# Sandwich of attention and a mixture-of-experts layer: the last batch's gating, the experts' weight splits and the shared expert's down products reordered

## The chip, the cores and the metric

One Trainium2 chip, one core. The metric is the time of one execution on the device in microseconds, the median of several. All engines (TensorE or PE, VectorE or DVE, ScalarE or ACT, GpSimd or POOL, SyncE or SP) run instruction lists of their own, each in its order, and are tied by counting semaphores that the kernel writes by hand.

## The reference

What is computed, with x of 4 batches x 512 tokens x 256 features, all float32:

```python
x = x + layernorm(attention1(layernorm(x)))        # 16 heads of 16, causal
h = layernorm(x)                                   # "hidden_states" of the second layer
hid = h + attention2(rmsnorm(h, ln1_w))            # 16 heads of 128, causal
x2 = rmsnorm(hid, ln2_w)
logits = x2 @ gate_w.T                             # 16 experts
probs = softmax(logits)
top_w, top_i = top_k(probs, 4);  top_w /= sum(top_w)
g, u = x2 @ w1[e]                                  # per expert, 176 wide each
routed = sum_e wfull[t, e] * ((silu(g) * u) @ w2[e].T)
shared = (silu(x2 @ sg.T) * (x2 @ su.T)) @ sh_down_w.T   # shared expert, 352 wide
x = x + layernorm(hid + routed + shared)
```

The experts are evaluated only for the tokens that chose them.

## The kernel before

The work goes through five stages: first attention, second attention (64 steps of one head of one batch), the shared expert, the routed experts (79 tiles of 128 rows), and the last normalisation. The second attention's output is accumulated in `hs`. While it works on batch b, the kernel also does the gating of batch b-1 in fixed steps (the `POST_...` constants): the rms norm, the transposes of x2, the logits, the softmax, the ranks (each expert's probability is compared with every other's), the places in the sorted row table `xs_rows`, and the scattering of rows. For the last batch (B-1 = 3) there is no later attention, so its gating is woven into the shared expert.

The shared expert is a loop over `SHARED` = 12 steps s, that is 4 batches x `SHR` = 3 slices of 128, 128 and 96 hidden features. In a step

- TensorE computes the gate and the up product (`shared_up(s)`, 12 matmuls of 512 columns into bank s%2 and bank 2+s%2), and a down product (`shared_down`, 12 matmuls of 256 columns into banks 6 and 7). Products of float32 data are made of three, with each operand split in a high and a low part (`_hi`, `_lo`).
- ACT takes silu of the gate into `gated[s%2]` (L1004), DVE multiplies it with the up product (L1407), ACT rounds it to the high part `hh_hi` (L1008), and POOL (steps 1 to 5, `shared_lo`, L733) or DVE (steps 0 and 6 to 11, L1417) subtracts to get the low part `hh_lo`. The down product of a slice needs both parts. The silu of step s >= 2 waits until the down product of step s-2 is done (`f_dn` >= s-1), since it overwrites `gated[s%2]`.
- After three slices DVE adds the down products to `hs` (L1414), which first needs `f_dn`, and `r_row` (the rows of that batch copied out).

Into the same loop are laid: the splits of the experts' first weights w1 in four quarters (c, gu), each a `w1_half` on ACT (L996, 128 x 2816) and a `w1_rest` on DVE (L1398, 128 x 2816, reading the raw and the high part in SBUF); and the last batch's gating: `norm_half` on ACT (L917) and `norm_half2` on DVE (L1245) write the normalised rows into `mid`, TensorE transposes them (`turn_x2`, L1709), ACT and DVE make xT from them (`take_x2`, L922 and L1250), TensorE does `logits` (L1716), DVE `logits_less_max` (L1258 to L1261), ACT `exp_logits` (L926), DVE `probabilities`, `compare` and `count_ranks` (L1265 to L1288), TensorE `counts` (L1731), DVE `places`, `rows_and_weights` (L1294 to L1315) and `table` (L1322 to L1334), which TensorE transposes (L1894) and DVE stores as `tab` (L1441).

POOL's list is not touched by the change: `root_of_squares`, `shared_lo(1)` to `(5)`, and then `send_tile` for the last batch's four tiles (tiles 12 to 15). A `send_tile` waits for the indices (`r_idx`), the weights (`r_w`) and the row fill of its tile (`r_row`, `fill_row` on ACT, L935), does two small copies (L681, L682) and issues four indirect DMAs (L684) that scatter rows to `xs_rows`. `fill_row` of tile 14 overwrites the buffer of tile 12 and waits until its four DMAs have landed; tile 15 waits for 13's.

SP loads the second expert weights w2 in four parts (`load_w2`, which wait for `f_u`); then waits for `tab` and for all rows sent (`x_sent`), loads tiles 0 to 3, the last part of w2, and then tiles 4 to 78 in turn. An expert tile goes through `turn_tile`, `take_x`, `up`, silu, `turn_h` and `down`; TensorE's loop does `up(i)`, `down(i-2)`, `turn_h(i-1)`, `turn_tile(i+2)`. The first `up` also waits for all four `w1_rest`, and the first `take_x` on ACT for the last down product (`f_dn` >= 12).

The order of everything in the loop is written out by hand with tests on s.

Of the kernel before, what the change touches and what calls it, by code (L numbers as in the profile page):

```python
# [31 lines left out]
def sandwich_kernel(nc, x_d, qkv1_d, wo1_d, qkvo2_d, ln_w_d, gate_d, moe_d, stack_d, out_d):  # L32
    B, TB, D = x_d.shape
    C = D // P
# [6 lines left out]
    E = gate_d.shape[2]  # L41
# [8 lines left out]
    SHR = -(-SHI // P)  # L50
# [22 lines left out]
    with ctx:  # L73
# [6 lines left out]
        bank = [ctx.enter_context(nc.psum_tensor(f"bank{i}", [P, 512], F32)) for i in range(8)]  # L80
# [248 lines left out]
        POST_ROW, POST_SEND = (11, 12, 13, 14), (12, 13, 14, 15)  # L329
        SHARED = B * SHR  # L330
        LO_POOL = 6

        def sends(when, n):

# [2 lines left out]
        def shared_rows(r):  # L337
            return min(P, SHI - P * r)
# [138 lines left out]
        def _(pool):  # L477
# [258 lines left out]
            root_of_squares(B - 1)  # L736
            for s in range(1, LO_POOL):
                shared_lo(s)
# [12 lines left out]
        def _(act):  # L751
# [168 lines left out]
            def take_x2(b, c, bank_):  # L920
                act.wait_ge(r_tp2, b * C + c + 1)
                act.activation(xT[:, b, HI, c, :], bank_[:, :], ACT.Copy, scale=ln_w[:, 1, c:c + 1]).then_inc(r_hi, 1)  # L922

            def exp_logits(b):
                act.wait_ge(r_sub, b + 1)
                act.activation(pr[:, :, :], lg[:, :, :], ACT.Exp).then_inc(r_exp, 1)  # L926

            def fill_row(b, j):

                t = TPB * b + j  # L930
                if t == 0:
                    act.wait_ge(d_const, 1)
                if t >= 2:
                    act.wait_ge(x_sent[t % 2], 16 * TOPK * (t // 2))
                act.activation(xrow[:, t % 2, :, 0:D], hs[:, t, :].unsqueeze(1).to_broadcast([P, TOPK, D]), ACT.Copy,  # L935
                               scale=midst[:, RR, j:j + 1]).then_inc(r_row, 1)
# [56 lines left out]
            def w1_half(c, gu):  # L993

                act.wait_ge(w_in[c], 16 * len(list(routed_pieces(gu, c))) * 2)
                act.activation(w1[HI][c][:, gu, :], w1_raw[c][:, gu, :], ACT.Copy, scale=ln_w[:, 1, c:c + 1])\  # L996
                   .then_inc(w_hi, 1)

            for s in range(SHARED):
                rows = shared_rows(s % SHR)  # L1000
                act.wait_ge(f_g, s + 1)
                if s >= 2:
                    act.wait_ge(f_dn, s - 1)
                act.activation(gated[0:rows, s % 2, :], bank[s % 2][0:rows, :], ACT.Silu).then_inc(f_silu, 1)  # L1004
                if s == 3:
                    exp_logits(B - 1)
                act.wait_ge(f_h, s + 1)
                act.activation(hh_hi[0:rows, s % 2, :], gated[0:rows, s % 2, :], ACT.Copy).then_inc(f_hh, 1)  # L1008
                if s == 0:
                    w1_half(0, 0)  # L1010
                    norm_half(B - 1)
                if s == 1:
                    for c in range(C):
                        take_x2(B - 1, c, bank[4 + c])
                    w1_half(0, 1)
                if s in (6, 7):
                    w1_half(1, s - 6)
                if s in (5, 6, 7, 8):
                    fill_row(B - 1, s - 5)

            def take_x(i):
                act.wait_ge(e_t, i + 1)
# [30 lines left out]
        def _(dve):  # L1053
# [202 lines left out]
            def logits_less_max(b, bank_):  # L1256
                dve.wait_ge(r_lg, b + 1)
                link(dve.tensor_reduce(lg[:, :, :], bank_[:, 0:2 * TPB * E].rearrange("p (t a e) -> p t e a", t=TPB, a=2),  # L1258
                                       AX.X, ALU.add))
                link(dve.tensor_reduce(col[:, :], lg[:, :, :], AX.X, ALU.max))  # L1260
                dve.tensor_tensor(lg[:, :, :], lg[:, :, :], wide(col[:, :]), ALU.subtract).then_inc(r_sub, 1)  # L1261

            def probabilities(b):
                dve.wait_ge(r_exp, b + 1)
                link(dve.tensor_reduce(col[:, :], pr[:, :, :], AX.X, ALU.add))  # L1265
                link(dve.reciprocal(col[:, :], col[:, :]))
                link(dve.tensor_tensor(pr[:, :, :], pr[:, :, :], wide(col[:, :]), ALU.mult))

            def compare(experts):

                above = []
                for e in experts:
                    own = pr[:, :, e:e + 1]
                    if e:
                        above.append(dve.tensor_tensor(rk[:, :, e, 0:e], pr[:, :, 0:e],
                                                       own.to_broadcast([P, TPB, e]), ALU.is_ge))
                    above.append(dve.tensor_tensor(rk[:, :, e, e:E], pr[:, :, e:E],
                                                   own.to_broadcast([P, TPB, E - e]), ALU.is_gt))
                link(*above)
# [116 lines left out]
            def w1_rest(c, gu):  # L1396
                dve.wait_ge(w_hi, 2 * c + gu + 1)
                dve.scalar_tensor_tensor(w1[LO][c][:, gu, :], w1_raw[c][:, gu, :], ln_w[:, 1, c:c + 1], f32(w1[HI][c][:, gu, :]),  # L1398
                                         ALU.mult, ALU.subtract).then_inc(w_lo, 1)

            for s in range(SHARED + 1):
                if s < SHARED:
                    rows = shared_rows(s % SHR)
                    dve.wait_ge(f_silu, s + 1)
                    dve.wait_ge(f_u, s + 1)
                    half = gated[0:rows, s % 2, :]
                    dve.tensor_tensor(half, half, bank[2 + s % 2][0:rows, :], ALU.mult).then_inc(f_h, 1)  # L1407
                if s and s % SHR == 0:
                    b = s // SHR - 1
                    dve.wait_ge(f_dn, s)  # L1410
                    dve.wait_ge(r_row, TPB * (b + 1))
                    for i in range(2):
                        two = hs[:, TPB * b + 2 * i:TPB * b + 2 * i + 2, :].rearrange("p j d -> p (j d)")
                        dve.tensor_tensor(two, two, bank[6 + i][:, :], ALU.add).then_inc(f_acc, 1)  # L1414
                if s == 0 or LO_POOL <= s < SHARED:
                    dve.wait_ge(f_hh, s + 1)
                    dve.tensor_tensor(hh_lo[0:rows, s % 2, :], gated[0:rows, s % 2, :], f32(hh_hi[0:rows, s % 2, :]),  # L1417
                                      ALU.subtract).then_inc(f_lod, 1)
                if s == 0:
                    norm_half2(B - 1)  # L1420
                if s == 1:
                    for c in range(C):
                        take_x2(B - 1, c, bank[4 + c])
                    w1_rest(0, 0)
                if s == 2:
                    logits_less_max(B - 1, bank[4])
                    w1_rest(0, 1)
                if s == 3:
                    probabilities(B - 1)
                    compare(range(0, 6))  # L1430
                if s == 4:
                    compare(range(6, E))
                    count_ranks(B - 1)
                if s == 5:
                    places(B - 1, bank[5])
                    rows_and_weights(B - 1)
                if s == 6:
                    table()
                if s == 7:
                    dve.wait_ge(r_tabT, 1)  # L1440
                    dve.tensor_copy(tab[0:1, :], bank[4][0:1, 0:2 * P]).then_inc(r_tabi, 1)  # L1441
                if s >= SHARED - 2 and s < SHARED:
                    w1_rest(1, s - SHARED + 2)

            def take_x(i):
                dve.wait_ge(e_xh, i + 1)
# [49 lines left out]
        def _(pe):  # L1496
# [375 lines left out]
                ins.then_inc(f_dn, 1)  # L1872

            pe.wait_ge(s_ok, SHR)
            for s in range(SHARED + 1):
                if s == SHR * (B - 1):
                    pe.wait_ge(r_lo, C * B)
                if s < SHARED:
                    shared_up(s)
                if s:  # L1880
                    shared_down(s - 1)
                if s == 1:
                    pe.wait_ge(b_acc, C * N2)
                    for c in range(C):
                        turn_x2(B - 1, c, bank[4 + c])
                if s == 2:
                    logits(B - 1, bank[4])
                if s == 5:
                    pe.wait_ge(r_lo, C * B)
                    counts(B - 1, bank[5])  # L1890
                if s == 7:
                    pe.wait_ge(r_tab, 1)
                    for i in range(2):
                        ins = pe.transpose(bank[4][0:1, P * i:P * (i + 1)], tabc[:, i:i + 1], ident[:, :])  # L1894
                    ins.then_inc(r_tabT, 1)
# [131 lines left out]
```

## Time and profile before

| | us |
|---|---|
| median of 3 runs | 1220.91 |
| lowest, highest | 1219.78, 1225.69 |
| the profiled execution's own time | 1221.95 |
| its span, first to last instruction | 1220.2 |

| engine | busy us | share of the span | instructions |
|---|---|---|---|
| TensorE matmuls | 1160.6 | 95% | 7868 |
| DVE | 846.3 | 69% | 2663 |
| ACT | 799.6 | 66% | 2069 |
| POOL | 580.7 | 48% | 844 |

Times of the profile are microseconds from the first instruction. A row of a timeline gives the start, the duration, the engine, the line of the kernel and the operation, then output <- input tiles, and in brackets how long the engine had been idle and what ended that. A line L1500 is that of a helper that issues nearly all matmuls. The shared expert runs from 923.6 us to about 991 us, the expert tiles follow. Durations of instructions that follow each other at once overlap by up to 0.1 us.

### The profile page before, as it was taken

The page shows a single profiled execution, that of the slowest core. Times are in us where ns is not written, and L with a number is a line of the kernel's source. Part 1 is how long each engine was busy: PE and PEld are TensorE (multiplying, and loading weights), DVE is VectorE, ACT ScalarE, POOL GpSimd, SP SyncE. Part 2 cuts the span into 40 slices and gives each one's busy share as a digit, 9 for nine tenths or more (in the row PEclk, how much of TensorE's full clock was granted, in tenths as well). Part 3 has the DMA queues.
Part 4 walks back from the last instruction along what each step waited for, and adds up shares of the span by engine and source line. Part 5 has one row for each costly group of instructions (what it writes and reads, how often), then busy time and mean ns, then how long its engine had stood idle before and what let it go on. Part 6 is the DMA issues. An engine that isn't in the chain of part 4 may idle for free.

```text
span 1220.2 us, 25017 instructions
## 1 busy us (share of the span) xinstructions
PE 1160.6 (95%) x7868; PEld 988.4 (81%) x7868; DVE 846.3 (69%) x2663; ACT 799.6 (66%) x2069; POOL 580.7 (48%) x844
## 2 busy tenths in 40 slices
PE   6999999899999999999999999999998879999986
PEld 5766566689999989999989999889986769999962
DVE  5778888576677667876677876668865755555535
ACT  3587888677778776778776787777786524444422
POOL 4063655454334444457343466334453446666650
PEclk9999999999999999999999999999999989999998
DMA  8965555256631211213121131211114237777766
GB/s 271 284 190 168 173 175 170 89 176 191 189 114 57 91 51 57 81 53 123 35 69 37 35 109 67 69 36 54 64 54 132 78 112 116 118 119 118 119 110 223
DMA packets 111779, 139.58 MB, mean 114 GB/s; under 512 B 11364, under 2 KB 94820, under 8 KB 111524
## 3 DMA queue, kind: packets, MB, share of 16 engines
q1 hardware_dynamic: 97204, 119.10, 32.2%
q0 software_dynamic: 14448, 18.88, 9.5%
q8 instruction: 68, 1.11, 0.4%
q14 instruction: 59, 0.48, 0.1%
HBM read 63.36 MB, written 61.87 MB: 103 GB/s over the span
## 4 chain that ended last, share of the span: by engine, by line
PE 76%; DVE 8%; ACT 6%; issue 4%; POOL 3%; DMA 2%; SPq 1%; POOLq 0%; ACTq 0%; DVEq 0%
PE bank L1500 56%; PE bank L1742 5%; PE bank L1926 5%; PE bank L1561 2%; DVE bank L1127 2%; PE bank L1597 2%; PE bank L1614 2%; POOL xs_rows L684 1%; PE bank L1604 1%; PE bank L1905 1%; PE bank L1936 1%; ACT pT L842 1%; POOL sum_rows L746 1%; ACT p L966 1%; DVE hs L1358 1%
## 5 line engine op out<-in xcount | busy, mean ns | idle before, releaser
L1127 DVE CUSTOM_DVE_ANT_0 bank<-bank,mask 128x512 f32<-128x512 f32 (+3 forms) x512 | 235.1, 522 | 42.3 <-PE bank L1500 21.6
L957 ACT ACTIVATE p<-bank,stat 128x512 f32<-128x512 f32 (+3 forms) x256 | 131.6, 527 | 127.0 <-DVE stat L1127 127.0
L537 POOL CAST w_hl<-raw_qkv 128x512 fp32r<-128x512 f32 x96 | 58.8, 613 | 301.9 <-DMA raw_qkv<-in_qkvo 154.2
L1500 PE MATMUL bank<-xT,w_hl 128*128 128x512 f32 x768 | 190.3, 396 | 0.0
L1500 PEld LDWEIGHTS bank<-xT,w_hl 128*128 128x128 f32 x768 | 142.2, 188 | 37.1 <-issue 2.0
L746 POOL DMA_INDIRECT sum_rows<-mid,goal x79 | 122.9, 1555 | 70.7 <-DVE mid L1464 68.1
L966 ACT ACTIVATE p<-p,stat 128x512 f32<-128x512 f32 (+3 forms) x256 | 123.1, 553 | 14.7 <-DVE stat L1361 14.7
L538 POOL TENSOR_TENSOR w_hl<-raw_qkv,w_hl 128x512 fp32r<-128x512 f32 x96 | 124.2, 1294 | 7.8
L1383 DVE TENSOR_TENSOR o<-bank,o 128x512 fp32r<-128x512 f32 x64 | 44.2, 690 | 109.4 <-ACT o L973 109.4
L1500 PE MATMUL bank<-pT,v 128*128 128x256 f32 (+2 forms) x576 | 117.1, 348 | 0.0
L1500 PE MATMUL bank<-k,q 128*128 128x512 f32 (+2 forms) x576 | 111.5, 337 | 2.5 <-ACT pT L950 1.7
L1500 PE MATMUL bank<-wo_hl,o 128*128 128x256 f32 x768 | 107.6, 289 | 3.6 <-DVE o L1383 1.4
L1500 PEld LDWEIGHTS bank<-w_hl,xT 128*128 128x128 f32 x768 | 98.7, 188 | 10.7 <-issue 5.5
L1500 PEld LDWEIGHTS bank<-k,q 128*128 128x128 f32 x576 | 96.9, 189 | 11.7 <-DVE k L1231 1.9
L1500 PE MATMUL bank<-w_hl,xT 128*128 128x256 f32 x768 | 101.4, 280 | 3.1 <-DVE xT L1250 3.1
L1500 PEld LDWEIGHTS bank<-wo_hl,o 128*128 128x128 f32 x768 | 95.9, 190 | 5.5 <-issue 3.2
L842 ACT ACTIVATE pT<-bank 128x512 f32<-128x512 f32 x160 | 85.3, 603 | 19.0 <-PE bank L1604 17.4
L1500 PE MATMUL bank<-w_hi,sh_hi 128*128 x316 | 96.9, 348 | 0.5 <-issue 0.4
L1345 DVE TENSOR_TENSOR pT<-bank,pT 128x256 fp32r<-128x256 f32 (+2 forms) x192 | 96.1, 550 | 0.4
L1500 PEld LDWEIGHTS bank<-pT,v 128*128 128x128 f32 x576 | 87.9, 189 | 3.2
L524 POOL TENSOR_SCALAR_AFFINE_SELECT pT<-pT 128x256 f32<-128x256 f32 x128 | 51.5, 407 | 70.2 <-ACT pT L842 65.7
L1358 DVE TENSOR_TENSOR hs<-hs,bank 128x512 f32<-128x512 f32 x128 | 81.9, 679 | 1.1 <-PE bank L1500 1.1
(248 smaller groups left out, 2561.3 us busy)
## 6 DMA issues: line engine op xcount, KB each, us to landing
raw_qkv<-in_qkvo SPq DMA_DIRECT2D x32, 768.0 KB, 5.3
xs_rows<-blank SPq DMA_DIRECT2D x32, 520.0 KB, 3.3
xs_rows<-blank SPq DMA_DIRECT2D x5, 2730.0 KB, 14.6
xrow<-xs_rows SPq DMA_DIRECT2D x79, 130.0 KB, 2.5
raw_o<-in_qkvo SPq DMA_DIRECT2D x32, 256.0 KB, 3.6
sum_rows<-blank SPq DMA_DIRECT2D x3, 2176.0 KB, 8.5
stk<-xT SPq DMA_DIRECT2D x96, 64.0 KB
stk<-k_hl SPq DMA_DIRECT2D x96, 64.0 KB
```

The source lines that it names most:

```text
L537: link(pool.tensor_copy(hi, raw))
L538: pool.tensor_tensor(lo, raw, f32(hi), ALU.subtract).then_inc(done, 1)
L746: pool.indirect_dma_start(sum_d[i % NSUM], bass.IndirectOffsetOnAxis(goal[:, i % NY:i % NY + 1], 0), yt[:, i % NY, :], None, compute_op=AL ...
L842: act.activation(pT1[:, s % 2, i, :], st1(s, i)[:, :], ACT.Exp).then_inc(a1_exp, 1)
L957: act.activation(p2[:, n % 2, POFF[qi]:POFF[qi + 1]], s2(t), ACT.Exp, scale=-1.0, bias=stat2[:, 0, n % 2, t:t + 1], accum_out=stat2[:, 1, ...
L966: act.activation(pt, pt, ACT.Copy, scale=stat2[:, 2, n % 2, t:t + 1]).then_inc(b_norm, 1)
L1127: return dve.tensor_tensor_reduce(scores, scores, mask[:, TB - scores.shape[1]:], scale=-1.0, scalar=-2.0 * MASKED, op0=ALU.add, op1=ALU.m ...
L1345: dve.tensor_tensor(pT2[:, LO, QOFF[kj]:QOFF[kj + 1]], bank[t][:, 0:TB - P * kj], f32(pT2[:, HI, QOFF[kj]:QOFF[kj + 1]]), ALU.subtract).th ...
L1358: dve.tensor_tensor(two, two, bank[4 + c][:, :], ALU.add).then_inc(b_acc, 1)
L1500: ins = pe.matmul(out, a, b, start=start and i == 0, stop=stop and i == len(pairs) - 1, **kw)
L1742: ins = pe.transpose(bank[t][:, P * (qi - kj):P * (qi - kj + 1)], p2[:, (n - 1) % 2, POFF[qi] + P * kj:POFF[qi] + P * (kj + 1)], ident[:, :])
L1926: ins = pe.matmul(bank[6 + i % 2][:, 0:D], ht[:, i % 2, P * h:P * (h + 1)], w2r[:, ds(expert[i], 1), h, :].rearrange("p a n -> p (a n)"), ...
```

## The change

It reorders the lists of TensorE, ACT and DVE in the shared expert's loop; no instruction is added or taken away.

- TensorE: the down product of a slice is issued two steps after its up product instead of one (the loop has a step more); the last batch's transposes move from step 1 to step 2, behind `shared_down(0)`; its logits move from step 2 to step 3, and stand ahead of `shared_down(1)`.
- ACT: `norm_half` from step 0 to step 1; `take_x2` from step 1 to step 2, now between silu and the rounding; `exp_logits` stays in step 3 but goes ahead of that step's silu; the four `w1_half` go from steps 0, 1, 6, 7 to steps 2, 4, 7, 8; the row fills from steps 5, 6, 7, 8 to 5, 6, 8, 9.
- DVE: `take_x2` from step 1 to step 2; `logits_less_max`, `probabilities` and the first compares stand at the head of step 3, the other compares and the count at the head of step 4, ahead of the products; the additions to `hs` move a step later; the four `w1_rest` go from steps 1, 2, 10, 11 to steps 7, 8, 9, 10.

```diff
+        SPLIT_W1, REST_W1, FILL_LAST = (2, 4, 7, 8), (7, 8, 9, 10), (5, 6, 8, 9)
...
             for s in range(SHARED):                                   # ACT
                 rows = shared_rows(s % SHR)
+                if s == 3:
+                    exp_logits(B - 1)
                 act.wait_ge(f_g, s + 1)
                 if s >= 2:
                     act.wait_ge(f_dn, s - 1)
                 act.activation(gated[...], bank[s % 2][...], ACT.Silu).then_inc(f_silu, 1)
-                if s == 3:
-                    exp_logits(B - 1)
+                if s == 2:
+                    for c in range(C):
+                        take_x2(B - 1, c, bank[4 + c])
                 act.wait_ge(f_h, s + 1)
                 act.activation(hh_hi[...], gated[...], ACT.Copy).then_inc(f_hh, 1)
-                if s == 0:
-                    w1_half(0, 0)
+                if s == 1:
                     norm_half(B - 1)
-                if s == 1:
-                    for c in range(C):
-                        take_x2(B - 1, c, bank[4 + c])
-                    w1_half(0, 1)
-                if s in (6, 7):
-                    w1_half(1, s - 6)
-                if s in (5, 6, 7, 8):
-                    fill_row(B - 1, s - 5)
+                if s in SPLIT_W1:
+                    w1_half(*divmod(SPLIT_W1.index(s), 2))
+                if s in FILL_LAST:
+                    fill_row(B - 1, FILL_LAST.index(s))
...
-            for s in range(SHARED + 1):                               # DVE
+            for s in range(SHARED + 2):
+                if s == 3:
+                    logits_less_max(B - 1, bank[4])
+                    probabilities(B - 1)
+                    compare(range(0, 6))
+                if s == 4:
+                    compare(range(6, E))
+                    count_ranks(B - 1)
                 if s < SHARED:
                     ...
-                if s and s % SHR == 0:
+                if s > SHR and s % SHR == 1:
                     b = s // SHR - 1
-                    dve.wait_ge(f_dn, s)
+                    dve.wait_ge(f_dn, s - 1)
...
-                if s == 1:
+                if s == 2:
                     for c in range(C):
                         take_x2(B - 1, c, bank[4 + c])
-                    w1_rest(0, 0)
-                if s == 2:
-                    logits_less_max(B - 1, bank[4])
-                    w1_rest(0, 1)
-                if s == 3:
-                    probabilities(B - 1)
-                    compare(range(0, 6))
-                if s == 4:
-                    compare(range(6, E))
-                    count_ranks(B - 1)
...
-                if s >= SHARED - 2 and s < SHARED:
-                    w1_rest(1, s - SHARED + 2)
+                if s in REST_W1:
+                    w1_rest(*divmod(REST_W1.index(s), 2))
...
-            for s in range(SHARED + 1):                               # TensorE
+            for s in range(SHARED + 2):
                 if s == SHR * (B - 1):
                     pe.wait_ge(r_lo, C * B)
                 if s < SHARED:
                     shared_up(s)
-                if s:
-                    shared_down(s - 1)
-                if s == 1:
+                if s == 3:
+                    logits(B - 1, bank[4])
+                if s >= 2:
+                    shared_down(s - 2)
+                if s == 2:
                     pe.wait_ge(b_acc, C * N2)
                     for c in range(C):
                         turn_x2(B - 1, c, bank[4 + c])
-                if s == 2:
-                    logits(B - 1, bank[4])
```

## Rows read from the trace of the kernel before

**Rows 1.** the chain of waits from 955 to 1003 us: start us, us, what

```profile
961.88 0.20 POOL xrow L681
...
985.89 2.44 DMA xs_rows<-xrow,idx
...
998.96 2.07 DMA xrow<-xs_rows
```

**Rows 2.** one line of the kernel, the sends: duration ns min/median/max

```profile
L684 POOL DMA_INDIRECT xs_rows<-xrow,idx x64: 956/964/3827, 538.5 to 985.9; - x64
```

**Rows 3.** POOL timeline, 920 to 1006: start, us, engine line op, tiles, [idle before]

```profile
939.80 4.16 POOL L733 TENSOR_TENSOR hh_lo<-gated,hh_hi 96x512 fp32r<-96x512 f32 x1 [5.04 <-ACT hh_hi L1008]
...
972.97 0.20 POOL L681 COPY xrow<-dst 128x4 int32<-128x4 int32 x1
...
979.01 1.17 POOL L684 DMA_INDIRECT xs_rows<-xrow,idx  x1 [0.28 <-POOL xrow L682]
...
981.76 3.83 POOL L684 DMA_INDIRECT xs_rows<-xrow,idx  x1 [0.30 <-issue]
```

**Rows 4.** DVE timeline, 920 to 1006

```profile
930.61 0.61 DVE L1245 TENSOR_SCALAR mid<-hs,midst 128x256 f32<-128x256 f32 x2 [1.78 <-POOL midst L673]
...
938.98 0.28 DVE L1258 TENSOR_REDUCE lg<-bank 128x64 f32<-128x128 f32 x1
...
946.94 0.21 DVE L1265 TENSOR_REDUCE col<-pr 128x4 f32<-128x64 f32 x1
...
950.79 0.18 DVE L1275 TENSOR_TENSOR ranks<-pr 128x24 bf16<-128x24 f32 x1
...
951.72 1.31 DVE L1277 TENSOR_TENSOR ranks<-pr 128x24 bf16<-128x24 f32 x1
...
955.54 0.19 DVE L1288 TENSOR_SCALAR msk<-lg 128x64 bf16<-128x64 f32 x1
...
961.58 0.17 DVE L1315 TENSOR_TENSOR wk<-posf,col 128x16 f32<-128x16 f32 x1
...
964.07 0.41 DVE L1322 TENSOR_TENSOR ranks<-run,thr 128x256 f32<-128x256 f32 x1
...
967.50 0.69 DVE L1407 TENSOR_TENSOR gated<-gated,bank 128x512 f32<-128x512 f32 x1
...
978.64 0.68 DVE L1417 TENSOR_TENSOR hh_lo<-gated,hh_hi 128x512 fp32r<-128x512 f32 x1
...
981.60 3.15 DVE L1398 SCALAR_TENSOR_TENSOR w_lo<-w_raw,ln_w,w_hi 128x2816 fp32r<-128x2816 f32 x1
...
989.71 1.27 DVE L1414 TENSOR_TENSOR hs<-hs,bank 128x512 f32<-128x512 f32 x2
```

**Rows 5.** ACT timeline, 920 to 1006

```profile
930.61 0.91 ACT L917 ACTIVATE mid<-hs,midst 128x256 f32<-128x256 f32 x2
...
962.39 0.63 ACT L1008 ACTIVATE hh_hi<-gated 128x512 fp32r<-128x512 f32 x1 [3.87 <-DVE gated L1407]
962.93 2.63 ACT L996 ACTIVATE w_hi<-w_raw,ln_w 128x2816 fp32r<-128x2816 f32 x1
...
971.29 1.13 ACT L935 ACTIVATE xrow<-hs,midst 128x1024 f32<-128x1024 f32 x1
```

**Rows 6.** ACT timeline, 1160 to 1221

```profile
1176.81 1.28 ACT L757 ACT_TABLE_LOAD   x1
```

**Rows 7.** TensorE timeline, 920 to 1006

```profile
944.01 0.38 PE L1500 MATMUL bank<-sh_hi,hh_hi 96*128 96x256 f32 x1 [2.56 <-POOL hh_lo L733]
...
967.76 0.48 PE L1500 MATMUL bank<-xT,sh_hi 128*96 128x512 f32 x1
...
970.61 0.28 PE L1500 MATMUL bank<-sh_hi,hh_hi 128*128 128x256 f32 x1
...
972.04 0.40 PE L1500 MATMUL bank<-xT,sh_hi 128*128 128x512 f32 x1
```

**Rows 8.** windows: stretch, busy us (count) of each engine, granted TensorE clock, DMA

```profile
945.50:949.00 3.50, 3.50 (x11) 2.73 (x10) 3.06 (x16) 1.88 (x2) 0.00 (x0) 0.51 0.00 0
```

## The prediction

> **What bounds the kernel now.** I read four views, in this order. First the page: TensorE is busy 95% of the span and leads the chain that ended last, but that is an average, and the change lies between the end of the second attention (922 us) and the first expert tiles. Second, the chain of waits of that stretch. From 961.88 to 985.89 us it is not TensorE but POOL, which issues the 16 scattering DMAs of the last batch (`send_tile`); the last one lands at 985.89 + 2.44 = 988.33, then SP issues four tile loads, the last weight loads and the load of tile 4, which lands at 998.96 + 2.07 = 1001.03, and from there TensorE runs tile after tile [rows 1]. So 12.7 us after the last send lands the steady expert loop begins, and the end of the sends sets the end of the kernel. Third, the timelines of POOL, DVE and ACT, for what releases the first send (`wk` on DVE, 961.58 [rows 4]) and what stretches the sends. Fourth, the windows, for TensorE's clock.
>
> What stretches a send: 64 of them take 0.964 us in the median and 3.83 at most [rows 2]. The long one starts at 981.76, 0.16 us after a `w1_rest` on DVE (981.60, 3.15 us, both tensor inputs in SBUF), and ends at 985.59, 0.84 us after that ends [rows 3, 4]. The same sum fits a small case: `hh_lo` on DVE ends at 979.32, the send that starts at 979.01 ends at 980.18, 0.86 us later. A POOL subtraction issued while `w1_rest(0,1)` runs (939.80) takes 4.16 us. I take the rule: a send that starts inside such a DVE operation ends 0.85 us after it, so each `w1_rest` among the sends costs 1.75 to 3.0 us (its 3.15 less up to 1.27, the spacing of sends, less 0.12), 2.4 on the average.
>
> The Trainium skill ("SBUF — State Buffer", section "SBUF: two separate sides") says that the port pair shared by DVE and GpSimd is an exclusive lock, taken by a DVE operation with two SBUF inputs against a GpSimd one that reads SBUF, and held for the whole instruction by whichever starts first. The stretched sends agree. By the same rule a `w1_rest` that meets a running send would wait up to one send (0.96) itself, which would add up to 1 us to the sum; this trace shows no such wait, so the sum leaves it out.
>
> **The change part by part.** Times below are those of the profiled execution. An `up` of TensorE takes 2.74 to 2.85 us, a `down` 1.43 [rows 7]; silu 0.58, the product on DVE 0.69, `hh_hi` 0.63, `w1_half` 2.63, a row fill 1.13, each 0.05 to 0.09 shorter where the next follows at once [rows 4, 5].
>
> *Up to the logits (even).* The first w1 half leaves ACT (it held norm_half until 930.61), but norm_half now stands behind `hh_hi` of step 1, which needs the product of step 1, and that is queued on DVE behind norm_half2 (930.61 + 0.61). So product 931.1 to 931.8, `hh_hi` to 932.5, norm_half to 933.3 instead of 931.5: 1.8 us later [rows 4, 5]. TensorE spends this time on up 2 and down 0 (to 933.4), then the transposes, then up 3 (to 937.05). ACT and DVE take x2 by 936.15 (before 935.4), the logits follow up 3 at once, and less-max starts at 938.94 against 938.98 [rows 4]. Cost nothing; up 3 is the cover, and without it the step would be 0.8 late.
>
> *From logits to ranks (gain 7.9).* Now the exponential comes before silu 3 and the probabilities before product 3. With the table loaded while ACT waits (at the end of the kernel the load stands at 1176.81, long before its instruction's data [rows 6]) (1.28 us) it ends at 940.0, 0.3 behind less-max, and DVE goes on at once. Before, product 3, the slow POOL subtraction (939.80 + 4.16, since `w1_rest` ran beside it), a TensorE stall and the addition to hs stood between, until 946.94 [rows 3 to 5]. After: probabilities and the first compares 940.04 to 941.9, product 3 when silu 3 is through its own table load (942.3 to 942.9), the other compares and the count 4.9 (950.79 to 955.73, in it 1.1 that one compare waits for POOL, 1.31 long among others of 0.18 [rows 4]): ranks at 947.8, before 955.73. The moved downs cost nothing here: TensorE runs gapless from 934 to 957, and the slow stretch at 945.5 (granted clock 0.51, the 1.2 GHz level, after the stall [rows 7, 8]) goes.
>
> *From ranks to the first send (4.5 given back).* Counts can start at 948.6, but DVE's product 4 and addition end at 949.6 and product 5 needs silu 5, and that is behind `w1_half(0,1)`, which step 4 now holds (949.0 to 951.6). A product, the places, rows and weights take 6.0 us (955.73 to 961.58 + 0.17 [rows 4]), so from silu 5's end at 952.2 they end at 958.3. The first send moves from 961.88 to 958.4: **3.4 us earlier**.
>
> *The sends (8.0 lost).* Before: 24.97 us, of it one lock of 2.86, so 22.1 free. All four `w1_rest` now stand at steps 7 to 10, all inside the sends; two were at 935 and 939, one after the sends. The table (964.07 to 967.50, 3.4 us [rows 4]) now ends at 963.7. TensorE has nothing to do between down 5 (957.2) and the transposes of the table at 963.8, 6.6 us; after the stall of 2.56 us that ended at 944.01 [rows 7] it ran 3.5 us at half clock, so up 8 will run slow, 2.85 + 0.9 to 2.4. Then down 6 ends near 970.2, and silu 8 now waits for it. Product 8 ends at 971.5, `hh_hi` at 972.1, `w1_half(1,1)` 974.7, fill 2 at 975.8. POOL: tile 12's sends 958.4 to 964.0, tile 13's 964.0 to 971.6 (one lock, `w1_rest(0,0)` at 966.4), then it waits for fill 2 until 975.9 (before, fill 2 ended at 971.29 + 1.13, just in time for tile 14's copies at 972.97 [rows 3, 5]). Two tiles free are 10.8 us (972.97 to 986.85 less 2.86 and 0.2), and `w1_rest(1,0)` near 978.3 and `w1_rest(1,1)` near 983.7 fall into them, 2.4 each: the last send ends at 975.9 + 10.8 + 4.8 = 991.5 instead of 986.85.
>
> **Sum: +4.6 us**: the chain behind the sends (SP's loads, 12.7 us) moves as it is. TensorE's own last `down` ends near 990 and DVE's last addition near 991.5 (before 989.71 + 1.27), both hidden behind the tile loads, which would arrive at 996. By bounds: with the full clock at up 8, fill 2 ends at 974.4 and the sends at 990.1 (+3.3); with half clock throughout up 8 and locks as long as the measured 2.86, +6.2. The profiled execution took 1221.95 against a median of 1220.91; I add to the median: **1225.5 us**.
>
> **The rivals.** *Locks absent (not slower).* If the 3.83 send had another cause (it is one case), only the wait for fill 2 is left: 974.4 to 975.9 plus 10.8 gives 985.2 to 986.7, -1.6 to -0.2: about 1220. For it: the long send is one case, and the median of 64 shows none. Against: the end 0.85 after DVE's fits twice. It decides from where the two locks behind fill 2 cost under 0.2 to 1.7 us together (986.85 less 10.8 less 975.9 or 974.4).
>
> *Everything late (slower by over 0.5%).* The exponential's table load does not run ahead (+1.3 at the ranks, +0.9 at fill 2), up 8 wholly at half clock (+1) and locks of 2.86 (+0.9): +7.5, 1228.4. For it: [rows 6] is another load, at another place. Against: like it, the exponential has a single wait.
>
> *Sends no longer the bound (faster).* If fill 2 came in time and DVE's `w1_rest` mostly missed the sends (starts of sends just ahead of them), POOL would end at 958.4 + 22.1 = 980.5, and the first expert tile would be held by DVE's last addition, 991.5, instead of the load at 991.5, then three tiles of 2.27 without waits: `up` 3 at about 998.7 instead of 1001.9, -3.2, 1217.7. It needs silu 8 not to wait for down 6, against the order.
>
> *The change does nothing there* is excluded: order alone moves 3.4 us at the first send.
>
> **How the numbers follow.** Forecast (+3.3 to +6.2) 0.57; locks absent 0.14; all late 0.18; sends not the bound 0.07; something I don't see that makes it faster by more 0.04. Half a per cent is 6.1 us, about what a measurement can tell from no change. All late is slower; the forecast, locks absent and sends not the bound lie within. So faster 0.04, same 0.78, slower 0.18. The range leaves out the far ends of both sides, 1218.5 to 1228.5 (half of sends not the bound, the unseen, and the upper part of all late, together under 2 in 10); the forecast's own is 1224.2 to 1227.1.
>
> **What would show it.** Right: less-max at about 938.9; ranks near 947.8; first send near 958.4; a TensorE gap of 6 us ahead of the table's transposes and a granted clock near 0.5 in the 3 to 5 us behind them; three or four sends over 2.5 us, each ending 0.85 after a `w1_rest`; POOL idle on `xrow` of fill 2; last send near 991.5. Wrong: sends of 0.96 beside `w1_rest`, fill 2 before 972, or a first expert `up` that waits for DVE instead of a load.

## The result and the profile after

Six runs of the changed kernel took 1229.97 us in the median (1228.83 to 1231.23), six of the kernel before 1220.78. The ratio is 1.0068, with 95% interval 1.0050 to 1.0087: slower by 0.68%, or 8 to 9 us, against a forecast of 4.6. The time lies 1.5 us above the range's upper end. The direction and most of the mechanism were right, the size was not.

The profiled execution of after took 1228.98 us (span 1227.2, mean granted clock 0.984, against 0.990 before), 7.0 us more in the span. The first product of the shared expert starts at 926.19 us (before 926.75), and times after it are compared from that product. In the 13 profiles of this document it starts between 925.80 and 928.47, though nothing ahead of it was edited; this scatter stands in the medians and not in times from the product. The first view is the chain that ended last (start us, us, what):

```profile
973.54 2.16 ACT w_hi L997
...
975.99 1.15 ACT xrow L936
977.28 0.19 POOL xrow L682
...
980.86 2.76 POOL xs_rows L685
...
985.22 3.07 POOL xrow L683
...
992.64 2.44 DMA xs_rows<-xrow,idx
...
1005.83 2.16 DMA xrow<-xs_rows
```

As in [rows 1], it goes through POOL's sends, SP's loads and the load of tile 4. The new piece is ahead of them: POOL now stands behind ACT's `w1_half(1,1)` (L997) and fill 2, the row fill of tile 14 (L936). POOL's timeline (start, us, engine line op, tiles, idle before):

```profile
968.04 3.04 POOL L685 DMA_INDIRECT xs_rows<-xrow,idx  x1 [0.30 <-issue]
...
977.28 0.19 POOL L682 COPY xrow<-dst 128x4 int32<-128x4 int32 x1 [4.92 <-ACT xrow L936]
...
979.30 1.26 POOL L685 DMA_INDIRECT xs_rows<-xrow,idx  x1 [0.30 <-issue]
980.86 2.76 POOL L685 DMA_INDIRECT xs_rows<-xrow,idx  x1 [0.30 <-issue]
...
985.17 3.11 POOL L683 COPY xrow<-wk 128x4 f32<-128x4 f32 x1
...
989.85 1.21 POOL L685 DMA_INDIRECT xs_rows<-xrow,idx  x1 [0.30 <-issue]
```

Three long spans answer to the one of [rows 3], and one of them is a copy of 4 elements a partition, which takes 0.19 elsewhere. DVE's timeline shows what each meets; `w1_rest(0,1)`, at 974.18 and not among these rows, falls into POOL's wait and holds nothing:

```profile
938.42 0.29 DVE L1257 TENSOR_REDUCE lg<-bank 128x64 f32<-128x128 f32 x1 [2.76 <-PE bank L1496]
...
947.30 0.19 DVE L1287 TENSOR_SCALAR msk<-lg 128x64 bf16<-128x64 f32 x1
...
948.00 1.27 DVE L1420 TENSOR_TENSOR hs<-hs,bank 128x512 f32<-128x512 f32 x2
953.04 0.68 DVE L1413 TENSOR_TENSOR gated<-gated,bank 96x512 f32<-96x512 f32 x1 [3.77 <-ACT gated L1007]
...
967.11 3.13 DVE L1397 SCALAR_TENSOR_TENSOR w_lo<-w_raw,ln_w,w_hi 128x2816 fp32r<-128x2816 f32 x1
...
979.63 3.15 DVE L1397 SCALAR_TENSOR_TENSOR w_lo<-w_raw,ln_w,w_hi 128x2816 fp32r<-128x2816 f32 x1
...
985.09 3.14 DVE L1397 SCALAR_TENSOR_TENSOR w_lo<-w_raw,ln_w,w_hi 128x2816 fp32r<-128x2816 f32 x1
```

The send at 968.04 ends at 971.08, 0.84 after the `w1_rest` that ends at 970.24; the one at 980.86 ends at 983.62, 0.84 after 982.78. The copy at 985.17 ends at 988.28, 0.05 after 988.23: a held copy needs no 0.85. TensorE's timeline has two stalls, and the windows (stretch; busy us of PE, PEld, DVE, ACT, POOL; granted clock; DMA share, GB/s) show the 1.2 GHz level behind both:

```profile
949.42 0.55 PE L1496 MATMUL bank<-sh_hi,hh_hi 128*128 128x256 f32 x1 [2.55 <-DVE hs L1420]
...
964.50 0.58 PE L1890 MATMUL bank<-ident,tabc 128*1 128x128 f32 x2 [3.42 <-DVE tabc L1333]
```

```profile
949.40:952.30 2.90, 2.88 (x15) 2.81 (x15) 0.00 (x0) 1.88 (x1) 0.71 (x1) 0.50 0.50 145
964.50:969.90 5.40, 5.40 (x15) 3.62 (x16) 5.40 (x6) 3.16 (x2) 4.51 (x6) 0.52 0.21 75
```

Added up from the first product on, the last send ends at +67.41 (before +60.10). The 7.31 are 2.04 gained at the first send's copies, 4.92 of waiting for fill 2, 4.27 more of held instructions, that is what sends and copies took beyond their usual 0.97 and 0.19 (7.57 in all, before 3.30) and 0.16 of small gaps. Tile 4's transposes come at +81.85 (before +74.33, so +7.52), and from there to the end both take the same: 219.16 and 219.12.

### The profile page after: what moved, and what is told of

The parts are those of the page before. It is cut to its first block, busy times and chain, and to the rows that moved or that the text cites. A ratio compares the mean times of both kernels' runs of the same rounds, so it can differ in the third digit from the quotient of the medians.

```text
span 1227.2 us, 25017 instructions
## 1 busy us (share of the span) xinstructions
PE 1163.8 (95%) x7868; PEld 991.6 (81%) x7868; DVE 846.5 (69%) x2663; ACT 799.6 (65%) x2069; POOL 581.7 (47%) x844
## 4 chain that ended last, share of the span: by engine, by line
PE 79%; DVE 9%; ACT 6%; issue 3%; DMA 2%; POOL 2%; SPq 1%; POOLq 0%; ACTq 0%; DVEq 0%
PE bank L1496 57%; PE bank L1738 5%; PE bank L1922 5%; PE bank L1557 2%; DVE bank L1126 2%; PE bank L1610 2%; PE bank L1593 2%; PE bank L1901 1%; PE bank L1600 1%; PE bank L1932 1%; ACT pT L843 1%; ACT p L967 1%; ACT stk L848 1%; DVE hs L1357 1%; POOL xs_rows L685 1%
```

## The experiments

Theories on record before the runs: the sends bound the kernel and are lengthened by the wait for fill 2 and by `w1_rest` (theory S); against it, the moved down products cost the time (T), or the slower clock alone. A lock is a `w1_rest` that holds up POOL. The table holds one profiled execution each, us from the first product; "held" is the excess of sends and of copies, "add" the end of the last addition to `hs`, "tile 4" its transposes. From there to the end it took 216.9 to 219.4 us, in e2_fill2_at7 221.0, so differences of tile 4 under 2 us need the medians. Most of that scatter is not in the tiles: from tile 4's transposes to the last `turn_h` it took 174.2 to 174.9 us in eleven of the profiles and 176.5 in e2_fill2_at7 and e3_table_at8, while the last stage behind it took 42.1 to 44.5.

| kernel | 1st copies | wait, fill 2 | held | sends end | add | tile 4 | ratio to before, 95% |
|---|---|---|---|---|---|---|---|
| before | 35.13 | 0 | 3.25+0.05 | 60.10 | 64.23 | 74.33 | |
| after | 33.09 | 4.92 | 4.50+3.07 | 67.41 | 68.33 | 81.85 | 1.0068, 1.0050 to 1.0087 |
| e1_rest_out | 33.85 | 6.19 | 3.55+2.88 | 68.30 | 66.10 | 82.77 | 1.0079, 1.0048 to 1.0110 |
| e2_fill2_at7 | 33.09 | 0 | 10.21+0.03 | 65.03 | 67.68 | 79.39 | 1.0067, 1.0043 to 1.0091 |
| e3_table_at8 | 33.03 | 2.88 | 4.07+3.31 | 64.98 | 64.65 | 79.31 | 1.0053, 1.0034 to 1.0072 |
| e4_rest_pieces | 31.89 | 4.85 | 4.47+0.35 | 63.20 | 68.23 | 77.52 | 1.0036, 1.0023 to 1.0048 |
| e5_add_early | 30.55 | 4.52 | 4.46+3.08 | 64.46 | 65.39 | 78.78 | 1.0041, 1.0023 to 1.0058 |
| e6_down_only | 36.32 | 0 | 0.18+0.07 | 58.24 | 68.55 | 75.50 | 0.9997, 0.9983 to 1.0011 |
| e7_splits_only | 31.09 | 0 | 5.31+5.65 | 63.75 | 64.43 | 78.35 | 1.0022, 1.0008 to 1.0037 |
| e8_no_locks | 31.92 | 1.81 (fill 3) | 0.38+0.02 | 55.94 | 67.27 | 78.55 | 1.0039, 1.0022 to 1.0057 |
| h1_best | 30.59 | 0 | 1.84+0.04 | 54.18 | 64.10 | 71.77 | 0.9968, 0.9954 to 0.9982 |
| h2_rest_at8 | 30.59 | 0 | 4.67+3.50 | 60.47 | 60.82 | 74.79 | 1.0010, 0.9995 to 1.0024 |
| h3_rest_back | 30.54 | 0 | 4.09+6.15 | 62.48 | 63.03 | 76.87 | 1.0042, 1.0027 to 1.0058 |

The intervals of e1_rest_out, e2_fill2_at7 and e3_table_at8 overlap widely with that of after, and that of e5_add_early at its end: what these edits did is read from the traces, and the medians alone do not show a gain.

**Four edits of after, one suspected cost each.** The first takes two `w1_rest` out of the sends' time:

```diff
-        SPLIT_W1, REST_W1, FILL_LAST = (2, 4, 7, 8), (7, 8, 9, 10), (5, 6, 8, 9)
+        SPLIT_W1, REST_W1, FILL_LAST = (0, 2, 7, 8), (2, 4, 10, 11), (5, 6, 8, 9)
```

> The changed kernel with SPLIT_W1 = (0, 2, 7, 8) and REST_W1 = (2, 4, 10, 11): two of the four w1_rest leave the sends, one comes late in them. Theory S (the end of the 16 sends on POOL sets the time; w1_rest locks POOL; POOL waits for fill 2): fill 2 stays at about 977, but behind it there is one lock instead of two to four, so the last send ends near 990.5 instead of 993.6, about 1227 us against 1230. Rival T (the cost is TensorE's: its stalls and the half-clock stretches of the down products a step later): those stay, so 1230.

It missed: 1230.02 us. Both late `w1_rest` met POOL all the same, because POOL still waited for fill 2 (6.19 us) and sent later. POOL's timeline, then DVE's:

```profile
937.09 1.30 POOL L734 TENSOR_TENSOR hh_lo<-gated,hh_hi 96x512 fp32r<-96x512 f32 x1 [2.10 <-ACT hh_hi L1012]
...
984.71 3.05 POOL L682 COPY xrow<-dst 128x4 int32<-128x4 int32 x1
...
989.46 4.15 POOL L685 DMA_INDIRECT xs_rows<-xrow,idx  x1 [0.30 <-issue]
```

```profile
937.28 4.06 DVE L1397 SCALAR_TENSOR_TENSOR w_lo<-w_raw,ln_w,w_hi 128x2816 fp32r<-128x2816 f32 x1
...
989.62 3.14 DVE L1397 SCALAR_TENSOR_TENSOR w_lo<-w_raw,ln_w,w_hi 128x2816 fp32r<-128x2816 f32 x1
```

The early `w1_rest` shows the other direction: POOL's subtraction had begun 0.19 before it, kept its 1.30, and DVE took 4.06, 0.92 more than 3.14. At 989.46 a send had begun 0.16 before DVE, and it is the send that was held, 4.15. "SBUF — State Buffer" of the Trainium skill (section "SBUF: two separate sides") says that whichever of the two starts first keeps the ports shared by DVE and GpSimd for its whole instruction. The subtraction agrees with that, the send does not.

```diff
-        SPLIT_W1, REST_W1, FILL_LAST = (2, 4, 7, 8), (7, 8, 9, 10), (5, 6, 8, 9)
+        SPLIT_W1, REST_W1, FILL_LAST = (2, 4, 7, 8), (7, 8, 9, 10), (5, 6, 7, 9)
```

> The changed kernel with the fill of tile 14 at step 7 instead of 8, all else equal. Theory S: POOL's wait of 4.9 us for fill 2 goes, a w1_rest now meets the sends of tile 14 (2.4 us back): about -2.5, 1227.5 us. Rival T: no change on TensorE, 1230.

The wait of 4.92 went, but now all four `w1_rest` met a send (10.21 us), so only 2.4 came back at the end of the sends: a wait and the locks are not two separate costs. The median (1230.46) shows no gain at all. The profile shows one reason: the tail from tile 4 took 221.03 instead of 219.16, and the clock fell once more in the expert tiles (window of this kernel, then the same stretch of after), where 1.6 of the difference lies:

```profile
1010.00:1015.00 5.00, 5.00 (x24) 4.29 (x24) 2.11 (x7) 1.63 (x5) 1.59 (x1) 0.72 0.53 114
```

```profile
1010.00:1015.00 5.00, 5.00 (x32) 4.59 (x31) 2.64 (x8) 2.25 (x7) 2.47 (x2) 1.00 0.72 139
```

The next kernel has such a fall too: a granted clock of 0.81 in the same window and 1.6 us more in the tiles. Its total from tile 4 does not show it (218.88), because its last stage took 42.3 us instead of 44.3.

```diff
-                if s == 7:            # transposes of the table, and its copy (two places)
+                if s == 8:
```

> The changed kernel with the table's transposes and its copy at step 8 instead of 7, so that TensorE does up 8 and down 6 while DVE makes the table. The 5 us stall of TensorE at 959.5 and the half clock behind it should go, silu 8 come 3.3 us earlier, fill 2 about 2 us earlier. Theory S: the sends follow fill 2, -2 us, about 1228. Rival T: all of the 5 us that up 8 and the stall cost comes back, 1225.

Moving the transposes behind up 8 took 2.04 of the wait and 2.5 at tile 4; 1228.37 us. TensorE's wait for the table did cost time at tile 4; that it costs time in the median is not shown.

```diff
-                dve.scalar_tensor_tensor(w1[LO][c][:, gu, :], ...).then_inc(w_lo, 1)
+                n = E * EI // 4
+                for i in range(4):
+                    some = slice(n * i, n * (i + 1))
+                    ins = dve.scalar_tensor_tensor(w1[LO][c][:, gu, some], ...)
+                ins.then_inc(w_lo, 1)
```

> The changed kernel with every w1_rest cut in four pieces of 704 columns (0.8 us each, some 0.3 us more in all). If POOL gets the port between two pieces, a send is held by at most one piece: theory S gives locks of under 0.9 instead of 1.8 to 3.1, about -3 us, 1227. If POOL doesn't get in between pieces, 1230, which would tell that the lock isn't given up between DVE instructions. Rival T: 1230 to 1231.

With 704 columns in place of 2816 the held copies went, 1225.83 us. The first held send did not get shorter: POOL's timeline, then DVE's, where the four pieces stand as one line:

```profile
966.46 3.43 POOL L685 DMA_INDIRECT xs_rows<-xrow,idx  x1 [0.30 <-issue]
...
979.60 1.42 POOL L685 DMA_INDIRECT xs_rows<-xrow,idx  x1 [0.31 <-issue]
```

```profile
965.51 3.52 DVE L1400 SCALAR_TENSOR_TENSOR w_lo<-w_raw,ln_w,w_hi 128x704 fp32r<-128x704 f32 x4
```

It stood through the rest of all four and ended 0.86 after them, while the later ones got through in 1.42. Of the 4.3 us gained at tile 4, 1.2 is not the edit's, as TensorE's timeline and window show:

```profile
949.06 0.36 PE L1500 MATMUL bank<-sh_hi,hh_hi 128*128 128x256 f32 x1 [2.57 <-DVE hs L1424]
949.25 0.28 PE L1500 MATMUL bank<-sh_hi,hh_lo 128*128 128x256 f32 x1
```

```profile
949.20:950.40 1.20, 1.20 (x11) 1.20 (x12) 0.00 (x0) 1.20 (x1) 0.55 (x1) 1.00 0.59 177
```

Down 3, the down product of step 3, starts behind the same stall as in after (2.57 us) and runs at full clock.

**The stall that the prediction missed.** The addition of batch 0 (`add_down`, the same two instructions) goes ahead of the rank count, and `w1_half(0,1)` into ACT's idle time before `hh_hi` of step 4:

```diff
                     compare(range(6, E))
+                    add_down(s)
                     count_ranks(B - 1)
...
-                if s > SHR and s % SHR == 1:
+                if s > SHR + 1 and s % SHR == 1:
```

> The changed kernel with the addition of batch 0's down products to hs ahead of the rank count (it stood behind it, and down 3 waits for it through f_acc: TensorE stood 2.55 us at 949.4 and ran at half clock behind it), and with w1_half(0,1) in ACT's gap before hh_hi of step 4. Theory S with the wait that I had missed: down 3 no longer waits, silu 5 comes 3 us earlier, the first send 2.4 us earlier (30.7 behind the first product instead of 33.1), and so do table and fill 2: about -2.5 us against the changed kernel, ratio to before about 1.0045. If the wait on the addition costs nothing, first send at 33.1 and 1.0068.

It hit: 1226.98 us, first send at +30.55 against 30.7. DVE's timeline:

```profile
946.98 1.28 DVE L1408 TENSOR_TENSOR hs<-hs,bank 128x512 f32<-128x512 f32 x2
...
951.58 0.68 DVE L1424 TENSOR_TENSOR gated<-gated,bank 96x512 f32<-96x512 f32 x1 [1.18 <-ACT gated L1007]
```

The mask of the ranks starts 1.2 later (+22.32 against +21.11 in after, the addition's 1.28), TensorE's wait ahead of down 3 shrinks from 2.55 to 0.46, and the first send comes 2.5 earlier, tile 4 by 3.1. The two edits were not run apart. The wait for fill 2 and the locks stay as in after.

**Single parts on the kernel before.** The downs and additions alone, and the splits alone:

```diff
-                if s and s % SHR == 0:
+                if s > SHR and s % SHR == 1:
-                    dve.wait_ge(f_dn, s)
+                    dve.wait_ge(f_dn, s - 1)
...
-                if s:
-                    shared_down(s - 1)
+                if s >= 2:
+                    shared_down(s - 2)
```

> The kernel before with only the down products (and the additions behind them) a step later. Rival T (the downs a step later cost TensorE stalls and half clock): slower by 3 us or more, ratio 1.003 or more. Theory S: the first send 1 to 2 us earlier, since the stall on hh_lo at 941 and the addition ahead of the probabilities go, one lock among the sends as before: ratio 0.999, between 0.998 and 1.001.

1221.55 us, no change, so T falls as the account of the whole. The stall is there in small: down 3 waits 1.32 us for the moved addition. That the ratio came out as expected is luck, since both steps behind it failed: the first send came 1.2 later and not 1 to 2 earlier, and the last two `w1_rest` came behind the sends, so nothing was held. The last send started at 983.80; DVE's timeline:

```profile
985.71 3.15 DVE L1398 SCALAR_TENSOR_TENSOR w_lo<-w_raw,ln_w,w_hi 128x2816 fp32r<-128x2816 f32 x1
...
993.81 1.27 DVE L1414 TENSOR_TENSOR hs<-hs,bank 128x512 f32<-128x512 f32 x2
```

The sends end 1.9 earlier than before and the time is the same: the addition, 4.3 later, has taken over, since DVE's first `take_x`, which TensorE's first `up` of the expert tiles needs, stands behind it, and tile 4 comes 1.2 later.

```diff
-                    w1_rest(0, 0)
...
-                    w1_rest(0, 1)
...
-                if s >= SHARED - 2 and s < SHARED:
-                    w1_rest(1, s - SHARED + 2)
+                if s in (7, 8, 9, 10):
+                    w1_rest(*divmod((7, 8, 9, 10).index(s), 2))
```

(and `w1_half` at steps 2, 4, 7 and 8)

> The kernel before with only the eight w1 splits moved to the changed kernel's steps (w1_half 2, 4, 7, 8; w1_rest 7, 8, 9, 10). Theory S: gating about 3 us earlier (DVE and POOL are free of w1_rest there), but four locks among the sends instead of one, some 6.5 us: +3 to +4 us, ratio 1.003, sends' locks 8 to 10 us in sum. Rival T: faster than before or even, as TensorE's order is the old one.

1224.87 us. The first send comes 4.0 earlier and the last ends 3.65 later, with no wait for fill 2. Each of the four meets POOL:

```profile
966.17 3.09 POOL L684 DMA_INDIRECT xs_rows<-xrow,idx  x1 [0.30 <-issue]
...
970.52 3.06 POOL L681 COPY xrow<-dst 128x4 int32<-128x4 int32 x1
...
976.55 3.85 POOL L684 DMA_INDIRECT xs_rows<-xrow,idx  x1 [0.30 <-issue]
...
981.68 2.97 POOL L681 COPY xrow<-dst 128x4 int32<-128x4 int32 x1
```

**Locks away, and the other bound.** After, with `SPLIT_W1, REST_W1, FILL_LAST = (0, 4, 7, 8), (1, 11, 12, 13), (5, 6, 7, 8)`:

> The changed kernel with no w1_rest among the sends (steps 1, 11, 12, 13; w1_half 0, 4, 7, 8) and the fills at 5 to 8. Times from the first product of the shared expert. Theory S: first send at about 33.1 as in the changed kernel, the 16 sends take 22.1 to 22.6 without a long one, last send end at 55 to 56 instead of 67.4; the kernel is then bound by DVE's three late w1_rest (about 9 us behind its last product), near the time before. If sends are stretched by something else than w1_rest (the rival that locks are absent), they take 25 us or more.

The sends ended at +55.94, where 55 to 56 was expected, 11.5 earlier than in after. Tile 4 came only 3.3 earlier and the kernel took 1226.48 us, not near the time before as expected, since DVE now has three `w1_rest` behind its products:

```profile
988.34 6.20 DVE L1397 SCALAR_TENSOR_TENSOR w_lo<-w_raw,ln_w,w_hi 128x2816 fp32r<-128x2816 f32 x2
994.47 1.27 DVE L1420 TENSOR_TENSOR hs<-hs,bank 128x512 f32<-128x512 f32 x2
995.66 3.14 DVE L1397 SCALAR_TENSOR_TENSOR w_lo<-w_raw,ln_w,w_hi 128x2816 fp32r<-128x2816 f32 x1
```

**A version that beats both.** e5_add_early, the table at step 8 as in e3_table_at8, and `(0, 4, 7, 8), (1, 7, 11, 12), (5, 6, 7, 8)`:

> The changed kernel with the addition and w1_half(0,1) as in e5, the table's transposes at step 8, the fills at 5 to 8, w1_half at 0, 4, 7, 8 and w1_rest at 1, 7, 11, 12: one w1_rest among the sends, one in a gap of DVE, two behind them. Theory S: first send 30.7 behind the first product, sends 22.1 free and one or two locks, last send end at 55 to 58 instead of 60.1 (before) and 67.4 (changed): faster than before by 2 to 5 us, ratio 0.996 to 0.998. The end of DVE's two last w1_rest and addition, at 62 to 64, may take over as the bound (it was 64.2 before); then -2. Rival T: the downs a step later keep it at or above 1.000.

1218.03 us, ratio to before 0.9968 (0.9954 to 0.9982). Eleven of its twelve executions took 1217.21 to 1220.34 us and one 1880.36, which no trace explains. One send is held and fill 2 is in time; DVE's two last `w1_rest` and the addition behind them are the bound, as the sends' end (+54.18) no longer is. POOL, then DVE, then the chain that ended last, which goes from DVE's additions over its first `take_x` (L1449) to the first `up` of the expert tiles:

```profile
965.99 2.69 POOL L685 DMA_INDIRECT xs_rows<-xrow,idx  x1 [0.30 <-issue]
...
979.82 0.97 POOL L685 DMA_INDIRECT xs_rows<-xrow,idx  x1 [0.31 <-issue]
```

```profile
964.69 3.15 DVE L1399 SCALAR_TENSOR_TENSOR w_lo<-w_raw,ln_w,w_hi 128x2816 fp32r<-128x2816 f32 x1
...
983.31 6.20 DVE L1399 SCALAR_TENSOR_TENSOR w_lo<-w_raw,ln_w,w_hi 128x2816 fp32r<-128x2816 f32 x2
```

```profile
983.31 6.20 DVE w_lo L1399 x2
989.51 1.20 DVE hs L1408 x2
990.71 0.35 DVE sh_hi L1449
...
991.19 2.12 PE bank L1502 x6
```

The same with `REST_W1` = (1, 7, 8, 12), to relieve DVE's end:

> As h1_best with the third w1_rest at step 8 (1, 7, 8, 12), where DVE stood idle for 3.15 us. One lock more among the sends (end 54.2 + 2.4 = 56.6), but DVE's tail 3 us shorter (add at 61 instead of 64.1). The sends are the bound again: tile 4 at about 70.8 instead of 71.8 or, by where full overlap starts, up to 2 us earlier than h1_best: ratio to before 0.995 to 0.997.

It missed, 1222.85 us: the `w1_rest` at step 8 held a copy (3.52), which moved the sends back until the last one met the `w1_rest` of step 12 (3.62). And with `REST_W1` = (7, 8, 9, 10) as in the changed kernel:

> As h1_best, but with the four w1_rest back at the changed kernel's steps 7, 8, 9, 10. It doubles the suspected cost alone in a kernel whose gating and fills are good: four locks, 7 to 10 us in sum, last send end at about 61 to 63 instead of 54.2, ratio to before near 1.000 to 1.002 (+4 us against h1_best). If the locks don't matter (rival T), the ratio stays at 0.997.

1225.23 us. Against h1_best only the places of the `w1_rest` differ, and the ratio to before goes from 0.9968 to 1.0042: 0.74% by them alone, with 8.4 us more of held instructions and no wait for fill 2 in either. In the profiles tile 4 comes 5.1 us later by it; the first product, ahead of all edits, came 1.8 later too, so a part of the 0.74% may be scatter.

## Why the prediction was wrong in size

**Up to the ranks: right.** From the first product on, less-max was forecast at 12.2 and came at 12.23. The exponential's table load did run ahead of its data, as ACT's timeline shows, and the mask of the ranks ended at 947.49, or +21.3, against +21.05.

```profile
937.86 1.28 ACT L927 ACT_TABLE_LOAD   x1
939.26 0.26 ACT L927 ACTIVATE pr<-lg 128x64 f32<-128x64 f32 x1
```

**Ranks to the first send: the step that failed.** The forecast said "The moved downs cost nothing here: TensorE runs gapless from 934 to 957". It followed the additions as work of DVE, but not as something TensorE waits for: down 3, the first of batch 1, needs banks 6 and 7 free (`f_acc`), and the addition that frees them now stands a step later, behind the rank count (948.00 to 949.27). TensorE idled 2.55 us and ran down 3 in 2.7 instead of 1.43. Silu 5 waits for down 3, as it overwrites that slice's `gated`, and stood 1.14 us beyond the end of `w1_half(0,1)`, which the forecast had taken as its only wait. ACT's timeline:

```profile
952.42 0.59 ACT L1007 ACTIVATE gated<-bank 96x512 f32<-96x512 f32 x1 [1.14 <-PE bank L1496]
```

Silu 5 ended at 953.01, product 5 began at 953.04, or +26.85 (forecast +25.5), and the send's copies at +33.09 (forecast +31.65): 1.4 late. e5_add_early, which takes away most of this wait and also `w1_half(0,1)` from ahead of silu 5, gave 2.5 us there; by the row above, at most some 1.1 of it is the addition's (an estimate).

**The wait for fill 2: right in kind, 1.9 late.** The transposes of the table came 1.25 late, as the first send did. Up 8 ran wholly at half clock, 5.14 us where the sum had taken 4.5: 0.64. Fill 2 ended at +50.94 against +49.05. POOL waited 4.92, forecast 4.3. TensorE's gap ahead of the transposes was 3.42 us and not 6.6, as TensorE came late out of the stall; the granted clock fell to 0.52 all the same.

**The locks: right, 0.8 too small.** Behind fill 2 they and the small gaps cost 5.6 instead of 4.8; the prediction priced sends alone, and a held copy loses 2.9 of the 3.1. The rule that a send ends 0.85 behind DVE's operation held in after four times, two of them beside short subtractions (971.08, 980.56, 983.62 and 991.06).

1.25, 0.64 and 0.77 are the 2.66 by which the last send missed its forecast of +64.75. That makes +7.3 in place of +4.6 at the sends. The forecast's upper bound of +6.2 had room for the slower up 8 and the longer locks; it had none for the 1.25, the stall that it had put at nothing. "Locks absent" is refuted by h3_rest_back, "sends no longer the bound" did not occur in after, but it is what e6_down_only, e8_no_locks and h1_best became. "Everything late" (+7.5) came nearest in size, in part by luck: two of its three terms were real (up 8 wholly at half clock, longer locks); the third, a late table load, was not, and the stall ahead of down 3 stood in its place.

**Open:** the medians differ by 9 us and the ratio by 8.3, the profile by 7.0; the 2.66 account for the profile alone. Three of the six runs of after lie at 1228.8 to 1229.4 (clock 0.983 and 0.984) and three at 1230.5 to 1231.2 (0.982 and 0.983). Three things that vary between single profiles are large enough for this: where the first product starts (by 2.7 us), the last stage (42.1 to 44.5 us), and the clock that falls again in the tiles (1.6 us, in e2_fill2_at7 and e3_table_at8). Which of them made the three slower runs no profile shows.

## What to carry to other kernels

When an addition out of an accumulator bank is moved, ask first who refills the bank: it is a wait of TensorE, and a stall can cost twice, by its length and by the clock behind it. Long DVE operations that read two SBUF tensors belong where POOL has nothing to send, and moving them moves the sends too, so check the new meetings and not the old ones. A stage with three limits (sends, a fill, the last addition) gives little for relieving one: e8_no_locks brought the sends forward by 11.5 us and tile 4 by 3.3.

## What the runs showed of the hardware that was not expected

- POOL's small copies are held like sends: 0.19 became 3.11 beside a `w1_rest` of 3.14.
- A send that began 0.16 before a `w1_rest` was held for 4.15, and DVE's operation kept its 3.14; POOL's subtraction that began 0.19 before kept its 1.30, and DVE took 4.06.
- Four shorter operations back to back need not let a send in: it was held for 3.43 once, and got through in 1.42 at others.
- The expert tiles from tile 4 on took 174.2 to 174.9 us in eleven profiles of 13, and 1.6 more in the two in which the granted clock fell in their first 10 us.
- The granted clock behind equal stalls (2.55 and 2.57 us, at the same place) was 0.50 in one execution and 1.00 in another.
